# Attention with bilinear keys and ternary feed-forward: both projections of a head pair behind the first burst, keys as 64-column products, and a new order of the transfer queue

## The reference, cut to what matters

```python
# _L0_attn_ref, x is [8, 1024, 256], 16 heads of 64
xn = layernorm(x) * gamma
q, k, v = xn @ Wq, *split(xn @ Wkv)                  # to heads
q = apply_rotary(q, cos, sin) * 64 ** -0.5
k = apply_rotary(k, cos, sin)
kt = einsum('bhnd,hde->bhne', k, W_bilinear)
sim = einsum('bhid,bhjd->bhij', q, kt)
out = einsum('bhij,bhjd->bhid', softmax(sim), v)     # then out @ Wo
x = x + out @ Wo
x = x + ffn(layernorm(x))                            # ternary weights, gelu
```

## Time and profile before

| | us |
|---|---|
| median of 3 runs | 3529.55 (3527.23 to 3529.97) |
| the profiled execution, its own time | 3532.51 |
| its span in the trace | 3530.7 |
| TensorE busy | 3439.5 (97%) |
| VectorE busy | 2691.1 (76%) |
| GpSimd busy | 2622.0 (74%) |
| ScalarE busy | 2312.7 (66%) |

### The profile page before, as it was taken

One profiled execution on the slowest core, in us unless ns is written; L12 is line 12 of the kernel. 1 busy time (PEld: TensorE's weight loads), 2 busy tenths in 40 slices (PEclk: granted clock), 3 DMA queues, 4 the chain that ended last, 5 costly groups with the idle time before them and its releaser, 6 DMA issues. The chain is left out here.

```text
span 3530.7 us, 71278 instructions
## 1 busy us (share of the span) xinstructions
PE 3439.5 (97%) x21154; PEld 2220.5 (63%) x21154; DVE 2691.1 (76%) x4429; ACT 2312.7 (66%) x4412; POOL 2622.0 (74%) x1279
## 2 busy tenths in 40 slices
PE   6999999999999999999999999999999997999999
PEld 4655555555555555555555555556666654888888
DVE  6677777777777767777777777777777777899998
ACT  2666666666677666666666766666766664555555
POOL 2888888888888888888888888888888894222222
PEclk7999999999999999999999999999999998999999
DMA  5223322232223323333332233222322223233332
GB/s 194 75 100 111 101 94 91 98 119 100 96 99 121 100 89 100 114 95 100 100 120 97 95 100 119 100 99 97 118 91 91 73 86 101 89 97 98 98 96 68
DMA packets 255089, 355.75 MB, mean 101 GB/s; under 512 B 40220, under 2 KB 163484, under 8 KB 250268
## 3 DMA queue, kind: packets, MB, share of 16 engines
q1 hardware_dynamic: 245532, 343.29, 29.5%
q10 hardware_dynamic: 9216, 8.39, 0.7%
HBM read 219.49 MB, written 62.12 MB: 80 GB/s over the span
## 5 line engine op out<-in xcount | busy, mean ns | idle before, releaser
L459 POOL TENSOR_TENSOR prob_sum<-prob_sum,prob 128x1024 f32<-128x1024 f32 x762 | 1876.2, 2462 | 300.2 <-ACT prob L538 251.0
L538 ACT ACTIVATE prob<-scores 128x512 f32<-128x512 f32 x2048 | 1073.2, 600 | 394.9 <-PE scores L820 381.2
L742 DVE TENSOR_REDUCE row_max<-max_scores 128x1 f32<-128x512 f32 x1536 | 987.4, 684 | 433.4 <-PE max_scores L866 417.6
L1032 PE MATMUL attn_out<-prob,v 128*64 128x512 f32 x4096 | 935.3, 598 | 0.0
L811 PE MATMUL scores<-q_hi,k_hi 64*128 64x512 f32 x2048 | 777.7, 417 | 11.4 <-ACT scores L509 6.8
L816 PE MATMUL scores<-q_hi,k_lo 64*128 64x512 f32 x2048 | 749.1, 395 | 3.9 <-issue 3.9
L820 PE MATMUL scores<-q_lo,k_hi 64*128 64x512 f32 x2048 | 751.2, 396 | 0.0
L1032 PEld LDWEIGHTS attn_out<-prob,v 128*64 128x64 f32 x4096 | 271.1, 136 | 549.1 <-issue 547.8
L866 PE MATMUL max_scores<-k_hi,q_hi 64*128 64x512 f32 x1536 | 578.3, 430 | 14.8 <-DVE row_max L742 10.7
L509 ACT ACTIVATE scores<-neg_max_seeds 128x512 f32<-128x512 f32 x1024 | 553.4, 603 | 11.8 <-DMA neg_max_seeds<-neg_max_halves 11.8
L811 PEld LDWEIGHTS scores<-q_hi,k_hi 64*128 64x128 f32 x2048 | 377.1, 185 | 282.0 <-issue 158.2
(11 more groups left out here) (148 smaller groups left out, 4890.1 us busy)
## 6 DMA issues: line engine op xcount, KB each, us to landing
rows<-rows SPq DMA_DIRECT2D x512, 128.0 KB, 2.0
neg_max_seeds<-neg_max_halves SPq DMA_DIRECT2D x128, 512.0 KB, 4.0
w_group<-w_parts SPq DMA_DIRECT2D x30, 1536.0 KB, 6.9
attn_normalised<-z_stage SPq DMA_DIRECT2D x128, 256.0 KB, 2.1
v<-attn_normalised SPq DMA_DIRECT2D x64, 512.0 KB, 4.1
sum_inverted_rows<-sums_inverted SPq DMA_DIRECT2D x126, 256.0 KB, 4.8
x_turned_parts<-x_tile_parts SPq DMA_DIRECT2D x49, 256.0 KB, 2.8
xt_batch<-x_turned_parts SPq DMA_DIRECT2D x7, 1792.0 KB, 10.7
```

Of the source, the lines that this page charges most:

```text
L459: nc.gpsimd.tensor_tensor(sums_of(k, half), a, prob[:, n % RING, :, :], ALU.add).then_inc(added, 1)
L538: nc.scalar.activation(prob[:, n % RING, e, :], S[e][n % 2][:, :], ACT.Exp).then_inc(exped[e], 1)
L742: nc.vector.reduce_max(mx[1 - u][:, e, n // 2, n % 2:n % 2 + 1], bank_of(e, jj)[:, :], axis=AX.X)\
L1032: nc.tensor.matmul(O[rows(e), :], V[k // 2 % 2][:, j, col:col + DH], prob[:, n % RING, e, :], start=j == 0, stop=j == 7).then_inc(pv_made[ ...
```

## The change

The line numbers of the changed kernel are higher by 3 to 15.

- **TensorE.** Quarter 0 now holds the projection of the keys, the transpose of the maxima of half 1 (of the pair that this span scores, so one span later than before), the projection of the queries, and the sums, which go to X[1] in place of M. Quarter 1 has the burst and the value products alone. The maxima of half 0 are turned in quarter 2, between the projection of the values and the transposes of x. In quarter 3 each bilinear key product becomes two, one for each head, with 64 columns of weights; no transpose follows.
- **VectorE.** Both rotations stand in quarter 0. The low part of the queries is made at the end of quarter 3, behind the low parts of the keys and ahead of the statistics of x and the next burst's maxima.
- **ScalarE.** Seeds are written right behind the exponentials of a quarter, and `max_row` moves with its transpose.
- **The transfer queue.** Behind the swap of the keys come `max_rows(t - 1, 1)`, the swap of the queries, the stores of z, the sums and `max_seeds(t - 1, 1)`; the long loads of x and of weights stand behind `max_seeds(t, 0)` and the store of the inverse.

```diff
@@ the transfer queue, span
                 if proj:
                     for c in two:
                         swap(K, t, c)
+                if attn:
+                    max_rows(t - 1, 1)
+                if proj:
+                    for c in two:
+                        swap(Q, t, c)
                 if k >= 2:
                     for h in two:
                         store_z(k - 2, t - 2, h)
+                if k >= 1:
+                    sum_columns(t - 1)
+                if attn:
+                    max_seeds(t - 1, 1)
...
                 if prep:
                     max_seeds(t, 0)
-                    max_rows(t, 1)
                 if k >= 1:
                     store_inverse(t - 1)
-                if prep:
-                    max_seeds(t, 1)
+                if proj and p % 2 and k < T - 6:
+                    wait(sp, v_made, 2 * (t + 2) + 2)
+                    at_rest()
+                if proj and has_tile(k) and p == PAIRS - 1:
+                    load_xt(b + 1)
...
                 if k >= 1:
                     load_inverse(t - 1)
+                if proj and p % 2 and k < T - 6:
...
+                    load_w((p // 2 + 2) % (PAIRS // 2), (p // 2) % 2)
@@ scalar, span
+                    if attn and q < 3:
+                        seed(t, q + 1)
+                    if q == 0 and attn:
+                        max_row(t - 1, 1)
                     if proj and q == 2:
...
+                    if q == 2 and prep:
+                        if has_tile(k):
+                            wait(act, x_turned, t + 3)
+                        max_row(t, 0)
@@ vector, span
                     if q == 0:
                         if proj:
                             rotate(t, K)
-                    if q == 1:
-                        if prep:
-                            wait(dve, hi_made[Q], t + 2)
-                            nc.vector.tensor_tensor(QL[1 - u][:, :], rot[Q][:, :], QH[1 - u][:, :], ALU.subtract)\
-                                .then_inc(lo_made[Q], 1)
-                        if proj:
                             rotate(t, Q)
...
                                 nc.vector.tensor_tensor(KL[u][:, cols(c)], src, KH[u][:, cols(c)], ALU.subtract)\
                                     .then_inc(lo_made[K], 1)
+                            wait(dve, hi_made[Q], t + 3)
+                            nc.vector.tensor_tensor(QL[u][:, :], rot[Q][:, :], QH[u][:, :], ALU.subtract)\
+                                .then_inc(lo_made[Q], 1)
                         if has_tile(k + 1):
                             statistics(t + 1, 1 - u)
@@ tensor, span
+                    if q == 0:
...
+                            project(t, K, 0, p, w, order, x_red[1], 16 * (t + 1) + 2)
+                            project(t, K, 1, p, w, order, x_red[1], 16 * (t + 1) + 3)
+                        if attn:
+                            wait(pe, x_red[1], 16 * (t + 1) + (4 if prep else 0))
+                            turn_max(t - 1, 1)
+                        if proj:
+                            project(t, Q, 0, p, w, order, sin_made[K], 2 * pp + 1)
+                            project(t, Q, 1, p, w, order, sin_made[K], 2 * pp + 2)
...
-                                nc.tensor.matmul((M if c == 0 else X[0])[:, :], WB[:, p, :], rot[K][:, cols(c)],
-                                                 start=True, stop=True).then_inc(kt_made, 1)
-                        if prep:
-                            turn_max(t, 1)
+                                for e in two:
+                                    nc.tensor.matmul((M if c == 0 else X[0])[rows(e), :], WB[:, p, rows(e)], rot[K][:, cols(c)],
+                                                     start=True, stop=True).then_inc(kt_made, 1)
```

More of the change, by code:

```diff
@@ L275, in rows, with turned_cols @@
             return slice(e * DH, (e + 1) * DH)
+        def turned_cols(h):
+            return slice(0, P) if h else slice(2 * P, 3 * P)
         def cols(c):
@@ L384, in span @@
                         sp.dma_start(dst, src).then_inc(late_const, 16)
-                if proj:
-                    for c in two:
-                        swap(Q, t, c)
-                if k >= 1:
-                    sum_columns(t - 1)
+                p = (k + 2) % PAIRS
+                if proj and has_tile(k + 1):
+                    wait(sp, x_normed, t + 2)
+                    at_rest()
+                    load_x(t + 1, k + 1, b + (k + 1) // PAIRS - k // PAIRS)
                 if prep:
@@ L553, in span @@
                                                  scale=gam[:, kt:kt + 1]).then_inc(x_hi, 1)
-                    if attn and q < 3:
-                        seed(t, q + 1)
                     if q == 0 and k >= 1:
                         copy_sums(t - 1)
-                    if q == 1 and prep:
-                        max_row(t, 0)
                     if k == T - 2 and q == 3:
@@ L570, in keys @@
                         def keys(c):
-                            wait(act, kt_made, 2 * (t + 2) + c + 1)
+                            wait(act, kt_made, 4 * (t + 2) + 2 * c + 2)
                             src = (M if c == 0 else X[0])[:, :]
@@ L870, in turn_max, with project @@
                 wait(pe, negm_made, 2 * (t + 1) + h + 1)
-                nc.tensor.transpose(X[1][:, 0:P], negm[:, :], ident[:, :]).then_inc(nm_turned, 1)
+                nc.tensor.transpose(X[1][:, turned_cols(h)], negm[:, :], ident[:, :]).then_inc(nm_turned, 1)
+            def project(t, x, c, p, w, order, free, count):
+                wait(pe, free, count)
+                base = 2 * P * (1 - x) + P * (p % 2)
+                for m, (xp, wp, kt) in enumerate(order):
+                    last = nc.tensor.matmul((M if c == 0 else X[0])[:, :], w[:, wp, kt, base:base + P], XT[:, xp, kt, cols(c)],
+                                            start=m == 0, stop=m == len(order) - 1)
+                last.then_inc(proj_made[x], 1)
             def sums(k, t):
@@ L877, in sums @@
                         i = 2 * h + e
-                        nc.tensor.matmul(M[32 * i:32 * i + 32, :], ones[:, 0:32], sums_of(k, h)[:, e, :], start=True, stop=True)\
+                        nc.tensor.matmul(X[1][32 * i:32 * i + 32, :], ones[:, 0:32], sums_of(k, h)[:, e, :], start=True, stop=True)\
                             .then_inc(l_made, 1)
@@ L988, in span @@
                             last.then_inc(x_turned, 1)
+                    if q == 2 and prep and not proj:
+                        wait(pe, x_red[1], 16 * (t + 1) + 12)
+                        turn_max(t, 0)
                     if k == T - 1 and q == 1:
```

124 lines of the change are left out of this document (42 added, 82 removed).

## The result

The changed kernel takes **3547.84 us** (median of 5 runs, 3542.13 to 3549.52), the kernel before 3529.55 in the same session: a ratio of **1.0052**, 95% interval 1.0038 to 1.0067. It is slower by 18.3 us. Forecast were 3547.5, with 0.65 on slower. The profiled execution has a span of 3546.0 us and 3547.84 of its own.

A forecast was written before the change was run, and what follows sets the result against it. TensorE, busy 97% of the span, was taken as the bound. From 3532.5 us profiled, +33 for 53 spans, +1, -10 queue and -6 ends gave 3550.5, or 3547.5 for the median; range 3490 to 3585.

The forecast's parts named there:

- Quarter 0, +2.82: Quarter 0: queries start where the sums stood, transpose hidden; two projection halves and a change of shape add 2.82 us.
- Quarter 1, -3.12: Quarter 1: only burst and value products remain, 8.08 us against 11.20, so -3.12 us.
- Quarter 2, -0.03 between -0.2 and +0.2: Quarter 2: a transpose adds 0.11 us, an earlier offset of x shortens the burst by 0.14; together -0.03.
- Quarter 3, -0.30: Quarter 3: transpose gone, key products become pairs of 64 columns at 0.43 us; 9.80 us against 10.10.
- paid once: Quarter 3: key pairs share the value products' shape, so the change of shape is paid once.
- The new wait, +1.25, bounds 0 and 2.3: End of quarter 3: VectorE's low part waits for GpSimd's sum, delaying the next burst's maxima; +1.25 us a span.
- Sum of a span: One span of attention: -0.63 us without the new wait, plus 1.25 with it, +0.6 us.
- The late seeds that I gave 0.2 us of margin: Half 1's seeds land at 21.3 us, ScalarE needs them at 21.5; waits in quarter 2 would show the forecast wrong.
- The queue, -10: Transfer queue at 7 batch boundaries: seeds now stand ahead of the long load, saving TensorE 10 us.
- The ends, -6: Span 62: sums' transfer goes first, cutting TensorE's 8 us wait; -6 between 0 and -8; start 0 within 3.
- The hidden low part at 3475: Rival: the low part gets in ahead of GpSimd's sum, no new wait, 61 spans at -0.63: 3475 us; 15%.
- Key products one after the other: Rival, quarter 3: the two heads' key products serialise, 1.1 us x 61 = +67, 3615 us; 3%.

The follow-up runs named there:

- the last experiment: The kernel before, with only the low part of the queries moved to quarter 3, behind the low parts of the keys: 3558.81 us, ratio 1.0083.
- the keys' experiments: Changed kernel with key products as whole 128-column products: 3548.42 us, 1.0063; kernel before with them as pairs of 64 columns: 3529.96 us, 1.0010.
- whole keys: The changed kernel with the bilinear keys again as one product of 128 columns a half: 3548.42 us, ratio 1.0063.
- the doubled keys: The changed kernel with the first half's pair of key products done twice in each span: 3553.7 us, ratio 1.0085.

## Why the prediction was right

**Quarter 0, +2.82.** Right: without the wait it is 15.13 us against 12.26, +2.87. The queries start where the sums stood, and the transpose is hidden.

**Quarter 1, -3.12.** 11.20 to 8.14, -3.06.

**Quarter 2, -0.03 between -0.2 and +0.2.** -0.07 in the median. The transpose cost the 0.11 that was estimated. The burst gave 0.19 where I took the middle of 0 and 0.29. In the last experiment the low part alone brings it: the offset of x is made 2.4 us before the quarter, and the burst takes 4.50.

**Quarter 3, -0.30.** -0.30. The 0.43 us a pair was right but is not what it was said to be worked out from, 3.58 / 8 = 0.45: in the changed kernel neighbouring pairs start 0.43 us apart, and the first and the last of a stretch add the rest. The count of shape changes, "paid once", was right for the sum and wrong for its parts, as the keys' experiments show.

**The new wait, +1.25, bounds 0 and 2.3.** This was the term that decided the sign, and its chain held link by link. GpSimd's five sums start 21.91 us into quarter 1 (forecast 21.9). The low part is ready 8.08 into quarter 3 (8.1), ends 0.91 into the burst (0.9), the first reduction comes at 1.72 (1.9), the fourth maximum product at 2.47 (2.64). The sum that it waits for is the third of the five, as forecast. The burst grew from 4.55 to 5.66 in this span, 1.11 us. So the mechanism was right and the term 0.14 us too large; most of that is the time from the low part's end to the first reduction, 0.81 us where I had taken 0.94.

**Sum of a span.** Forecast +0.62, measured +0.57 in the two spans shown. What I did not see is that the chain absorbs: late seeds and whole keys vanish in it, and three quarters of the doubled keys. That made the forecast more robust than it deserved. The late seeds that I gave 0.2 us of margin did come late, 30 times, one of the signs that I had named for a wrong forecast, and they cost nothing, since quarter 0 shrank by as much.

**The queue, -10.** In the kernel before, the spans at the boundaries and those behind them stand 9.2 us above the others over six batches; after, they stand with the others. The size was right. Its cause as I put it, "now the seeds are ahead", was half of it: that order alone costs 53 us, and it needs the seeds' move to the next span.

**The ends, -6.** -5.0 in all between the two profiles, but the term is not confirmed: errors cancel in it, and the profile of the kernel before was long at both ends. The 8 us that TensorE waited in span 62 went, and 3.7 more of that quarter (20.12 to 8.38). But its quarter 0 grew from 9.07 to 14.27 and that of span 63 from 8.82 to 14.87. From span 62 on it is -2.4. The start, for which I had taken 0 within 3, gave -3.0 at the first full span. Kernels with the same two stretches as the kernel before give 82.2 to 87.2 us for the start and 633.4 to 634.6 for the end, and the change's 83.7 and 633.9 lie among them. So what the change itself gives at the ends is near nothing, where I had -6: the 8 us of waiting in quarter 3 of span 62 were worth little, since the two longer quarters 0 took them back. The 3 us by which the profile of the kernel before exceeded its median, taken off in my sum, are of the size of its long start.

**The rivals.** The hidden low part at 3475: its condition was not met, by the 0.9 us of margin that were stated (the low part starts 0.84 us after the sum has). Its price was too good by some 20 us: with the low part given to GpSimd and nothing else changed the ratio is 0.9903, 3495 us on the scale of the kernel before. Only with the seeds moved as well is it 0.9869, 3483. Key products one after the other: excluded, the two heads' products start within 0.01 us of each other, and such pairs come at 0.43 to 0.45 us. The direction and the mechanism were forecast; that the sum came out within 1 us of the median is luck at this precision: the terms missed by 0.14 us x 53 = 7 us in one place, by about 6 the other way at the ends, and by less in others.

## What to carry to other kernels

In these kernels an operation on VectorE with two SBUF operands, beside a GpSimd that added without a gap, cost up to 2.2 us more than its own time, nearly a whole sum of 2.4 (a product of z took 2.87 where it takes 0.68 alone), and a short one waited as a long one did. Place such an operation where GpSimd is idle, give it to GpSimd, or keep it away from the first thing that TensorE waits for. Before paying for a late transfer or a longer product, ask whether a later wait in the same period is tied to another engine: if so the repair gains nothing until that wait is gone, and then it suddenly does. And an order in a queue that looks wrong may be held by when its data is made: move the data first.

## What the runs showed of the hardware

A VectorE operation on 16 columns, with two operands in SBUF, took 1.59 us beside GpSimd's sums; in that run it took 0.43 at the least. VectorE, once waiting, got in between two sums of a gapless series, and the series was longer by just VectorE's own time (13.12 us for five sums instead of 12.05).

Reductions out of PSUM, and products with one operand in PSUM and one in SBUF, kept their 0.69 us beside the same sums (all 512 products of the rotations in the changed kernel took 0.68 to 0.69), so here the rotations could lie anywhere and the low part could not. Two products of 512 columns with both operands in SBUF took 1.28 us together beside an idle GpSimd and 5.05 beside its sums.

A wait of 5.9 us on TensorE was followed by 5.2 us at a granted clock of 0.54, and the twelve products in them took 5.15 us in place of 3.10: the wait cost 2 us on top of itself.

With the key products in 64 columns instead of 128, the time up to a lone 128-column transpose and the time from it to the 64-column value products were about 0.05 us longer each; without that transpose, a key stretch of whole products behind which the value products change the shape was 0.20 us longer than one of pairs.
